# Masked products of two token tiles in one block on TensorE, with y and z a step later, and idle transposes in three waits

## The chip, the cores and the metric

The program runs on one core of a Trainium2 chip. The metric is the device time of one execution in microseconds (us), as the median of several runs. The engines are PE (TensorE; PEld is its weight load), DVE (VectorE), ACT (ScalarE), POOL (GpSimd) and SP (SyncE, which issues the DMAs).

## What is computed

Four blocks follow each other on a residual stream `x` of 1024 tokens (4 sequences of 256) by 512 columns: a retrieval attention, a layer of 8 experts, a state-space mixer, and a layer of 4 experts. The third takes most of the time. Cut to what matters:

```
proj = layernorm(x) @ in_proj_w.T                 # gate, x, B, C, dt
xBC  = silu(causal_conv4(proj's x, B, C) + conv_b)
dt   = softplus(dt + dt_bias);  x_dt = x * dt
Lmat = exp(segment_sum(A * dt))                   # per head, within a chunk of 128 tokens
M      = (C @ B.T) * Lmat
Y_diag = M @ x_dt                                 # within the chunk
Y_off  = C @ (B * decay).T @ x_dt * exp(cumsum)   # across the two chunks of a sequence
y = Y_diag + Y_off + D * x
z = y * silu(gate) * norm_w                       # and y's mean square, for the row's scale
out = (z @ out_proj_w.T) * rsqrt(mean(y^2) + eps)
```

There are 128 heads of 64 channels in 8 groups, and each group has its own B and C.

## The kernel before, in words

Every large matmul is done in three passes: each operand is split into a high and a low part of a rounded type, and high*high, high*low and low*high are added up (`three_pass`, lines 203 to 205). ACT makes a high part by a copy, POOL or DVE a low part by a subtraction.

The mixer (`ssm_block`) walks over 8 groups. A group has 16 **steps** `s`: its 16 heads are two halves of 8 (`half`), and each half passes over 8 token tiles `t` of 128 tokens. A "lead" of half a group (g = -1, steps 8 to 15) runs ahead, and the last group has no projections in its second half. Each engine has its own `step(g, s, kind)` with its instructions in a fixed order; they meet through counting semaphores. What a step holds, by engine:

- **PE**: `turn(s + 1)` transposes the next tile of x (line 1827, 4 instructions, bank 6); `diag(s)` is the masked product, 8 matmuls of 64 columns of weights, one for each head, which write to the upper and the lower half of the partitions of bank 4 in turn (line 1837; the trace has two records for each); in odd steps `across(s)` does the product over chunks for a pair of tiles (line 1854, bank 5); `project(m)` makes one of 18 projection tiles of a group, 24 matmuls of 512 columns (lines 203 to 205, banks 0 to 3 in turn); `add_up(s - 1)` multiplies z of the tile before by the output weights, 12 matmuls of 512 columns into bank 7 (lines 1865, 1866 with z's high part, line 1869 with its low part). At the end of a group `within` (line 1916) and line 1963 form C*B for the next group.
- **DVE**: adds bank 7 to the accumulator (line 1569), scales the transposed x by dt (`times_dt`, line 1580), adds three taps of the convolution where the tile has one (`taps`, line 1558), scales the product over chunks (line 1641), makes y (lines 1653, 1663), z (line 1669), and masks the decays of tile s + 2 (`mask`, line 1602).
- **ACT**: takes projection s - 1 out of its bank (line 1300 or 1308), rounds the weights of tile m + 2 (line 1288), at the second tile of a half the output weights (line 1333, which waits for the last `add_up` of the half before), makes the decays of tile s + 2 (line 1321 eight times, line 1326 once, and a table load before it), applies silu to a convolved tile (line 1312), squares y (line 1394), and makes z's high part (line 1397).
- **POOL**: the low part of the weights (line 1215) and of z (line 1236), the sums of squares (1239 to 1245), and x scaled to the end of the chunk (1225).
- **SP**: the loads. A buffer of decays is loaded again when `diag_done` says that its tile was used.

So in the kernel before the masked product, y and z of tile s stand in step s, and the product of z with the output weights in step s + 1. The tables that place the projections are these (`has_tile` leaves out what a kind of group does not have):

```python
PROJECTED = [[n] for n in range(10)] + [[10, 11], [12], [13, 14], [15], [16], [17]]
EARLY = [[-1]] + [[n] for n in range(10)] + [[11], [12], [14], [15], [16]]
LATE = [[]] * 10 + [[10], [], [13], [], [], []]
```

Before the mixer and in each expert layer a layer norm is done (`norm_tensor`, `norm_vector`, `norm_scalar`): statistics and a square root on DVE and ACT, and then for each of 8 token tiles the normalised tile is transposed on PE (line 194), and split by ACT (line 182) and DVE (line 171). Blocks are separated by a barrier of all engines.

Of the kernel before, what the change touches and what calls it, by code (L numbers as in the profile page):

```python
# [174 lines left out]
def norm_scalar(nc, act, n, xh, between=None, after=None):  # L175
# [4 lines left out]
    for t in range(NT):  # L180
# [3 lines left out]
        if after:  # L184
            after(t)

# [387 lines left out]
def experts_block(nc, sems, tag, x, xh, xl, ident, bank, w, n, *, experts, rank, top2, scaling, split_low=False,  # L574
# [5 lines left out]
    with ExitStack() as ctx:  # L580
# [30 lines left out]
        with nc.Block() as block:  # L611
# [111 lines left out]
            def _(pe):  # L723
# [22 lines left out]

                norm_tensor(nc, pe, n, after=lambda t: products(t - 1) if t >= 1 else None)
# [3 lines left out]
                base(3)  # L751
                for hf in range(2):
# [26 lines left out]
def ssm_block(nc, ctx, sems, n, x_saved, ident, bank, acc, xh, xl, xdt, w_bufs, w_in, w_dt, par, dt_bias, a_log, w_out,  # L779
              ncs_dram, ecs_dram, units_dram, ffn, out):  # L780

# [244 lines left out]

    def has_tile(kind, m):

        return kind != "last" if m >= LEAD else kind != "lead"
# [37 lines left out]
    with nc.Block() as block:  # L1067
        @block.sync
        def _(sp):
# [88 lines left out]
            def step(g, s, kind):  # L1158
# [17 lines left out]
                if s % 2 == 1 and own(kind) and ahead(kind, s + 4):  # L1176
                    sp.wait_ge(y_ready, at(g, s))
                    load_e(g, s + 4)
# [12 lines left out]
        def _(pool):  # L1191
# [36 lines left out]

            def step(g, s, kind):
                t = s % NT  # L1230
                for m in EARLY[s] + LATE[s]:
                    if has_tile(kind, m) and has_tile(kind, m + 2):
                        w_low(g, m + 2)
                if own(kind):
                    pool.wait_ge(zh_ready, at(g, s))
                    nc.gpsimd.tensor_tensor(z_l[:, s % 2, :, :], zg[:], f(z_h[:, s % 2, :, :]),  # L1236
                                            ALU.subtract).then_inc(zl_ready, 1)
                    pool.wait_ge(sq_ready, at(g, s))
                    nc.gpsimd.tensor_tensor(ysq[:, 0:2, :], ysq[:, 0:2, :], ysq[:, 2:4, :],
                                            ALU.add).then_inc(sq_pair, 1)  # L1240
                    pool.wait_ge(sq_pair, g * STEPS + (s + 1))
                    nc.gpsimd.tensor_tensor(sq_acc[:, t, :], sq_acc[:, t, :], ysq[:, 0, :],
                                            ALU.add).then_inc(sq_first, 1)
                    pool.wait_ge(sq_first, g * STEPS + (s + 1))
                    nc.gpsimd.tensor_tensor(sq_acc[:, t, :], sq_acc[:, t, :], ysq[:, 1, :],
# [560 lines left out]
        def _(pe):  # L1806
# [113 lines left out]
            def step(g, s, kind):  # L1920
                if ahead(kind, s + 1) and s != STEPS - 1:
                    turn(g, s + 1)
                if own(kind):
                    diag(g, s)
# [192 lines left out]
```

## Time and profile before

| what | us |
|---|---|
| median of 3 runs | 1738.97 (1738.46 to 1739.18) |
| the profiled execution, by its own time | 1737.69 |
| its span, first to last instruction | 1735.9 |
| PE busy in the span | 1684.0 |
| ACT, DVE, POOL busy | 1269.4, 1190.5, 732.2 |
| stretch of the 8 groups, about | 290 to 1683 |

A row of the timeline gives the start, the length, the engine, the line and the operation, what is written and read, and how many instructions were merged. A matmul's record is longer than the distance to the next, since they are pipelined: a 512-column matmul lasts some 0.39 us and the next starts 0.23 us after it. So the distances between starts are what counts on PE. PEclk is the clock granted to PE, as a share of full speed: 1.00 is 2.4 GHz and 0.50 is 1.2 GHz.

### The profile page before, as it was taken

What the parts mean: (1) busy time and instruction counts of PE and PEld (TensorE: products, weight loads), DVE (VectorE), ACT (ScalarE), POOL (GpSimd) and SP (SyncE); (2) the same over time, 40 slices, a digit from 0 to 9 for tenths busy, and PEclk for the clock granted to TensorE, in tenths of its full rate; (3) what the DMA queues carried; (4) which work ended last, traced back from release to release, by engine and by line L of the source; (5) the groups of instructions that cost most, each with busy time, mean ns of one, the idle gap of its engine ahead of it and who ended that gap; (6) DMA issues with size and microseconds to landing.
All of it is one profiled execution on the core that took longest, in us unless ns stands there. A gap on an engine that the chain in (4) does not pass through costs nothing.

```text
span 1735.9 us, 26827 instructions
## 1 busy us (share of the span) xinstructions
PE 1684.0 (97%) x9484; PEld 1378.6 (79%) x9484; DVE 1190.5 (69%) x1846; ACT 1269.4 (73%) x2171; POOL 732.2 (42%) x792
## 2 busy tenths in 40 slices
PE   6998799999999999999999999999999999999999
PEld 5876577888888888888888888888888888888877
DVE  5665676767676767667776767676767676767785
ACT  4333148987888779877987798778887889688851
POOL 3553122544344334443444444434443444344470
PEclk9998799999999999999999999999999999999999
DMA  4320225423232323332333232323232233223311
GB/s 170 109 68 1 75 65 159 122 93 105 86 112 85 117 74 111 95 109 83 113 93 107 78 110 88 116 88 109 94 110 78 86 115 104 90 79 115 105 70 49
DMA packets 98564, 166.46 MB, mean 96 GB/s; under 512 B 11616, under 2 KB 49888, under 8 KB 96768
## 3 DMA queue, kind: packets, MB, share of 16 engines
q1 hardware_dynamic: 98432, 164.75, 29.7%
q8 instruction: 76, 1.25, 0.3%
q14 instruction: 56, 0.46, 0.1%
HBM read 158.43 MB, written 6.29 MB: 95 GB/s over the span
## 4 chain that ended last, share of the span: by engine, by line
PE 81%; DVE 4%; ACT 2%; issue 1%; DVEq 0%; ACTq 0%
PE bank L203 15%; PE bank L205 15%; PE bank L204 15%; PE bank L1837 7%; PE bank L1865 7%; PE bank L1866 7%; PE bank L1869 7%; PE bank L1854 4%; PE bank L1827 3%; PE bank L1916 1%; DVE m_xc L1558 1%; DVE m_gate L1558 0%; PE bank L1845 0%; ACT m_mt L1321 0%; DVE m_xc L1492 0%
## 5 line engine op out<-in xcount | busy, mean ns | idle before, releaser
L203 PE MATMUL bank<-xh,w_h 128*128 128x512 f32 x1152 | 463.3, 402 | 3.4 <-DVE m_xc L1558 2.9
L205 PE MATMUL bank<-xh,w_l 128*128 128x512 f32 x1152 | 451.8, 392 | 0.0
L204 PE MATMUL bank<-xl,w_h 128*128 128x512 f32 x1152 | 449.4, 390 | 0.0
L1236 POOL TENSOR_TENSOR m_z_l<-m_zg,m_z_h 128x512 fp32r<-128x512 f32 x128 | 177.6, 1387 | 568.6 <-ACT m_z_h L1397 568.6
L1321 ACT ACTIVATE m_mt<-m_mt,m_unit 128x128 f32<-128x128 f32 x1024 | 312.1, 390 | 0.0
L1215 POOL TENSOR_TENSOR w_l<-w_raw,w_h 128x512 fp32r<-128x512 f32 x144 | 187.7, 1303 | 230.9 <-ACT w_h L1288 230.9
L1569 DVE TENSOR_TENSOR x<-x,bank 128x512 f32<-128x512 f32 x128 | 87.8, 686 | 264.5 <-PE bank L1869 264.5
L203 PEld LDWEIGHTS bank<-xh,w_h 128*128 128x128 f32 x1152 | 216.8, 188 | 55.7 <-issue 13.6
L205 PEld LDWEIGHTS bank<-xh,w_l 128*128 128x128 f32 x1152 | 216.5, 188 | 47.3
L1558 DVE SCALAR_TENSOR_TENSOR m_xc<-bank,m_par_conv,m_xc 128x1020 f32<-128x1020 f32 (+2 forms) x192 | 244.6, 1274 | 10.4 <-ACT m_xc L1300 5.4
L204 PEld LDWEIGHTS bank<-xl,w_h 128*128 128x128 f32 x1152 | 217.1, 188 | 41.7
L1865 PE MATMUL bank<-m_wo_h,m_z_h 128*128 128x512 f32 x512 | 203.8, 398 | 1.3 <-DVE x L1569 1.3
L1866 PE MATMUL bank<-m_wo_l,m_z_h 128*128 128x512 f32 x512 | 202.5, 396 | 0.0
L1602 DVE TENSOR_TENSOR m_mt<-m_mt,m_cb 128x1024 f32<-128x1024 f32 x128 | 156.9, 1225 | 26.1 <-ACT m_mt L1326 26.0
L1837 PE MATMUL bank<-m_mt,xdt 128*64 128x128 f32 x2048 | 140.1, 279 | 0.1
L1869 PE MATMUL bank<-m_wo_h,m_z_l 128*128 128x512 f32 x512 | 138.5, 392 | 0.0
L1326 ACT ACTIVATE m_mt<-m_mt 128x1024 f32<-128x1024 f32 x128 | 135.8, 1061 | 2.2
L1653 DVE SCALAR_TENSOR_TENSOR m_y<-m_xc,m_par_dn,bank 128x128 f32<-128x128 f32 x480 | 133.9, 342 | 1.5 <-PE bank L1837 1.5
L1837 PEld LDWEIGHTS bank<-m_mt,xdt 128*64 128x64 f32 x2048 | 109.2, 136 | 21.5 <-issue 20.5
L1580 DVE TENSOR_TENSOR xdt<-bank,m_unit 128x512 f32<-128x512 f32 x128 | 87.8, 686 | 49.5 <-issue 48.6
L1326 ACT ACT_TABLE_LOAD x93 | 119.3, 1283 | 1.6
L1865 PEld LDWEIGHTS bank<-m_wo_h,m_z_h 128*128 128x128 f32 x512 | 96.1, 188 | 24.2 <-ACT m_z_h L1397 1.3
(275 smaller groups left out, 2781.0 us busy)
## 6 DMA issues: line engine op xcount, KB each, us to landing
m_mt<-ncs_rows SPq DMA_DIRECT2D x128, 512.0 KB, 3.7
w_raw<-w_in SPq DMA_DIRECT2D x144, 256.0 KB, 3.0
m_wo_raw<-w_out_in SPq DMA_DIRECT2D x64, 256.0 KB, 5.1
m_e<-ecs_rows SPq DMA_DIRECT2D x128, 128.0 KB, 3.5
a_wo_raw<-wo_in SPq DMA_DIRECT2D x8, 1024.0 KB, 4.9
x<-x_in SPq DMA_DIRECT2D x8, 256.0 KB, 4.6
a_wq_raw<-wq_in SPq DMA_DIRECT2D x8, 256.0 KB, 4.1
x_saved<-x SPq DMA_DIRECT2D x1, 2048.0 KB, 9.1
```

The source lines that it names most:

```text
L203: nc.tensor.matmul(out, ah, bh, start=first, stop=False)
L204: nc.tensor.matmul(out, ah, bl, start=False, stop=False)
L205: return nc.tensor.matmul(out, al, bh, start=False, stop=last)
L1215: nc.gpsimd.tensor_tensor(w_l[:, m % 2, :, :], w_raw[:, m % W_BUFS, :, :], f(w_h[:, m % 2, :, :]), ALU.subtract).then_inc(w_split, 1)
L1236: nc.gpsimd.tensor_tensor(z_l[:, s % 2, :, :], zg[:], f(z_h[:, s % 2, :, :]), ALU.subtract).then_inc(zl_ready, 1)
L1321: last = nc.scalar.activation(mt[:, s % ROW_BUFS, h, :], mt[:, s % ROW_BUFS, h, :], ACT.Relu, bias=own_row)
L1326: nc.scalar.activation(slot, slot, ACT.Exp, scale=-1.0).then_inc(decay_ready, 1)
L1558: ins = nc.vector.scalar_tensor_tensor(out=dst[:, :, back:], in0=src[:, :, 0:length - back], scalar=par_conv[:, w:w + 1], in1=dst[:, :, ba ...
L1837: last = nc.tensor.matmul(bank[row:row + SP_, 4, (h // 2) * P:(h // 2 + 1) * P], xdt[:, s % 2, h * SP_:(h + 1) * SP_], mt[:, s % ROW_BUFS, ...
L1865: nc.tensor.matmul(bank[:, 7, :], z_h[:, s % 2, ct, :], wo_h[:, ct, :], start=ct == 0, stop=False)
L1866: nc.tensor.matmul(bank[:, 7, :], z_h[:, s % 2, ct, :], wo_l[:, ct, :], start=False, stop=False)
L1869: last = nc.tensor.matmul(bank[:, 7, :], z_l[:, s % 2, ct, :], wo_h[:, ct, :], start=False, stop=ct == CT - 1)
```

## The change

1. **Steps are paired** (`paired`: all but the second half of the last group). In an odd step PE does `diag(s - 1)` and `diag(s)` one after the other, the even one into bank 4 and the odd one into bank 5; in an even step it does none. `across` moves to bank 7, which it shares with `add_up`.
2. **y and z are made a step later**: DVE, ACT and POOL do tile s - 1 in step s, DVE ahead of `times_dt` and the taps, ACT after the decays but ahead of silu. `add_up(s - 1)` keeps its place in step s. In the last group's second half tile s is made in step s again; its first step makes tiles 7 and 8.
3. **The end of a group**: `within(0)`, `within(1)` and the matmuls of line 1963 stand together, between the two halves of projection 16, in step 14; step 15 does both its masked products first.
4. **POOL** makes z's low part after the first tile's weights and ahead of the second tile's, in the two steps that have two.
5. **`turn_idle`** puts transposes of the identity on PE, 30 of them ahead of the first expert layer's norm and of the mixer's norm, and 24 after `base(3)` in the first expert layer, ahead of the wait for `hw_ready`. Nothing reads them.

The diff, cut to its core:

```diff
+def turn_idle(nc, bank, ident, count, spare=7):
+    for _ in range(count):
+        nc.tensor.transpose(bank[:, spare, 0:P], ident[:], ident[:])
...
+                turn_idle(nc, bank, ident, 30)
                 norm_tensor(nc, pe, n, after=lambda t: products(t - 1) if t >= 1 else None)
                 products(NT - 1)
                 base(2)
                 base(3)
+                pe.wait_ge(a_read, NT)
+                turn_idle(nc, bank, ident, 24, spare=3)
...
+    def paired(kind, s):
+        return not (kind == "last" and s >= NT)
+
+    def masked_in(kind, s):
+        if not own(kind):
+            return []
+        if paired(kind, s):
+            return [s - 1, s] if s % 2 == 1 else []
+        return [s]
+
+    def made_in(kind, s):
+        if not own(kind):
+            return []
+        if paired(kind, s):
+            return [s - 1] if behind(kind, s - 1) else []
+        return [s - 1, s] if s == NT else [s]
...
             # SP
-                if own(kind) and ahead(kind, s + ROW_BUFS):
-                    sp.wait_ge(diag_done, at(g, s))
-                    load_rows(g, s + ROW_BUFS)
+                for done in masked_in(kind, s):
+                    if ahead(kind, done + ROW_BUFS):
+                        sp.wait_ge(diag_done, at(g, done))
+                        load_rows(g, done + ROW_BUFS)
...
             # POOL, step
-                for m in EARLY[s] + LATE[s]:
+                for m in EARLY[s]:
                     if has_tile(kind, m) and has_tile(kind, m + 2):
                         w_low(g, m + 2)
+                for made in made_in(kind, s):
+                    split_and_square(g, made)
+                for m in LATE[s]:
+                    if has_tile(kind, m) and has_tile(kind, m + 2):
+                        w_low(g, m + 2)
...
             # ACT, step: after decay(g, s + 2), ahead of silu
+                if paired(kind, s):
+                    for made in made_in(kind, s):
+                        square_and_high(g, made)
                 for m in EARLY[s]:
                     if has_tile(kind, m) and is_conv[m % TILES]:
                         silu(g, m)
...
             # DVE, step: ahead of times_dt and taps
+                if paired(kind, s):
+                    for made in made_in(kind, s):
+                        make_y(g, made)
+                        make_z(g, made)
+                    if own(kind) and s % 2 == 1:
+                        scale_across(g, s, kind)
                 if ahead(kind, s + 1) and s != STEPS - 1:
                     times_dt(g, s + 1)
...
             # PE, diag
-                pe.wait_ge(y_ready, at(g, s - 1))
+                by_tensor = g == LAST and s >= NT
+                to_bank = 4 if by_tensor else 4 + s % 2
+                pe.wait_ge(y_ready, at(g, s - 1 if by_tensor and s > NT else s - 2))
...
             # PE, step
-                if own(kind):
-                    diag(g, s)
+                for ready in masked_in(kind, s):
+                    diag(g, ready)
+                if own(kind) and s % 2 == 1:
+                    across(g, s, kind)
                 todo = [m for m in PROJECTED[s] if has_tile(kind, m)]
+                for m in todo[:1]:
+                    project(g, m, 0)
+                    if s == STEPS - 2 and kind != "last":
+                        within(0).then_inc(cb_first_done, 1)
+                        within(1).then_inc(cb_last_done, 1)
...
+                    project(g, m, 1)
```

The order on PE, in an even and the following odd step of a middle group (`m_xc` is x, `m_mt` the masked decays, `m_cb_across` and `m_xdd` the product over chunks, `m_z_l` z's low part). Before, the end of one `add_up` and the next step's first instructions, for an odd step:

```order
L1869 MATMUL bank<-m_wo_h,m_z_l 128x512 x4
L1827 MATMUL bank<-ident,m_xc 128x128 x4
L1837 MATMUL bank<-m_mt,xdt 64x128 x8
L1854 MATMUL bank<-m_cb_across,m_xdd 128x128 x4
L203 MATMUL bank<-xh,w_h 128x512
```

An even step has the same without the row of line 1854. Now, an odd step:

```order
L1953 MATMUL bank<-m_wo_h,m_z_l 128x512 x4
L1901 MATMUL bank<-ident,m_xc 128x128 x4
L1915 MATMUL bank<-m_mt,xdt 64x128 x16
L1935 MATMUL bank<-m_cb_across,m_xdd 128x128 x4
L210 MATMUL bank<-xh,w_h 128x512
```

The 8 masked matmuls of the even step have moved behind it, into one block of 16, and the even step goes from line 1901 straight to line 210.

The order on ACT, in the first group's steps 0 and 1 (`m_mt` the decays, `m_ysq` the squares, `m_z_h` z's high part, `m_wo_h` the output weights). Before, from the decays of step 0:

```order
L1321 ACTIVATE m_mt<-m_mt,m_unit 128x128 x8
L1326 ACT_TABLE_LOAD
L1326 ACTIVATE m_mt<-m_mt 128x1024
L1394 ACTIVATE m_ysq<-m_y 128x512
L1397 ACTIVATE m_z_h<-m_zg 128x512
L1308 ACT_TABLE_LOAD
L1308 ACTIVATE m_gate<-bank 128x1024
L1288 ACTIVATE w_h<-w_raw 128x512
L1333 ACTIVATE m_wo_h<-m_wo_raw,m_par_dn 128x512 x4
L1321 ACTIVATE m_mt<-m_mt,m_unit 128x128 x8
```

Now:

```order
L1365 ACTIVATE m_mt<-m_mt,m_unit 128x128 x8
L1370 ACT_TABLE_LOAD
L1370 ACTIVATE m_mt<-m_mt 128x1024
L1352 ACT_TABLE_LOAD
L1352 ACTIVATE m_gate<-bank 128x1024
L1332 ACTIVATE w_h<-w_raw 128x512
L1377 ACTIVATE m_wo_h<-m_wo_raw,m_par_dn 128x512 x4
L1365 ACTIVATE m_mt<-m_mt,m_unit 128x128 x8
L1370 ACT_TABLE_LOAD
L1370 ACTIVATE m_mt<-m_mt 128x1024
L1410 ACTIVATE m_ysq<-m_y 128x512
L1413 ACTIVATE m_z_h<-m_zg 128x512
```

z's high part of the first tile has moved behind a projection's eviction, the output weights and a whole set of decays.

## Rows read from the trace of the kernel before

**Rows 1.** Windows: engines' busy us (count), PEclk, DMA; the groups' stretch

```profile
260.00:1700.00 1440.00, 1431.77 (x8295) 1176.00 (x8296) 1010.51 (x1514) 1177.69 (x2044) 640.47 (x728) 1.00 0.31 99
```

**Rows 2.** Timeline, PE, an odd step from 902.61 and an even one from 913.42

```profile
902.61 0.60 PE L1827 MATMUL bank<-ident,m_xc 128*128 128x128 f32 x4
903.14 1.09 PE L1837 MATMUL bank<-m_mt,xdt 128*64 128x128 f32 x16
904.16 1.16 PE L1854 MATMUL bank<-m_cb_across,m_xdd 128*128 128x128 f32 x8
...
910.64 0.40 PE L1865 MATMUL bank<-m_wo_h,m_z_h 128*128 128x512 f32 x1
...
913.42 0.60 PE L1827 MATMUL bank<-ident,m_xc 128*128 128x128 f32 x4
...
915.32 0.39 PE L204 MATMUL bank<-xl,w_h 128*128 128x512 f32 x1
...
920.56 0.40 PE L1865 MATMUL bank<-m_wo_h,m_z_h 128*128 128x512 f32 x1
```

**Rows 3.** Groups by line: busy us, mean ns, idle before; the masked products

```profile
L1837 PE MATMUL bank<-m_mt,xdt 128*64 128x128 f32 x2048 | 140.1, 279 | 0.1
```

**Rows 4.** Timeline, PE: a `turn` with no masked product behind it

```profile
827.22 0.60 PE L1827 MATMUL bank<-ident,m_xc 128*128 128x128 f32 x4
...
827.89 0.39 PE L1866 MATMUL bank<-m_wo_l,m_z_h 128*128 128x512 f32 x1
```

**Rows 5.** Timeline, ACT, around the even step at 913.42

```profile
912.28 2.44 ACT L1321 ACTIVATE m_mt<-m_mt,m_unit 128x128 f32<-128x128 f32 x8
...
917.52 0.61 ACT L1397 ACTIVATE m_z_h<-m_zg 128x512 fp32r<-128x512 f32 x1
```

**Rows 6.** Timeline, PE and ACT, step 1 of a middle group

```profile
840.39 0.60 PE L1827 MATMUL bank<-ident,m_xc 128*128 128x128 f32 x4
...
840.64 2.56 ACT L1333 ACTIVATE m_wo_h<-m_wo_raw,m_par_dn 128x512 fp32r<-128x512 f32 x4 [0.66 <-issue]
...
848.35 0.62 ACT L1397 ACTIVATE m_z_h<-m_zg 128x512 fp32r<-128x512 f32 x1
```

**Rows 7.** Timeline, ACT and PE, steps 0 and 1 of the first group

```profile
301.12 1.06 ACT L1326 ACTIVATE m_mt<-m_mt 128x1024 f32<-128x1024 f32 x1
...
303.23 1.28 ACT L1308 ACT_TABLE_LOAD   x1
304.52 1.03 ACT L1308 ACTIVATE m_gate<-bank 128x1024 f32<-128x1024 f32 x1
...
309.13 0.40 PE L1865 MATMUL bank<-m_wo_h,m_z_h 128*128 128x512 f32 x1
```

**Rows 8.** Timeline, PE and ACT, step 8 of the last group

```profile
1632.20 0.60 PE L1827 MATMUL bank<-ident,m_xc 128*128 128x128 f32 x4
...
1634.66 0.48 PE L1865 MATMUL bank<-m_wo_h,m_z_h 128*128 128x512 f32 x1
...
1634.28 1.06 ACT L1326 ACTIVATE m_mt<-m_mt 128x1024 f32<-128x1024 f32 x1
```

**Rows 9.** Windows, as rows 1: the three stretches at half clock ahead of the groups

```profile
143.70:153.80 10.10, 6.64 (x25) 5.85 (x26) 4.71 (x17) 2.21 (x4) 0.27 (x8) 0.50 0.01 3
...
181.20:187.90 6.70, 6.33 (x18) 4.45 (x17) 4.42 (x8) 1.20 (x2) 0.00 (x0) 0.50 0.00 0
...
205.10:218.70 13.60, 8.14 (x29) 6.28 (x30) 11.16 (x29) 6.64 (x11) 4.76 (x8) 0.50 0.73 269
```

**Rows 10.** Windows of line 1988 alone (transposes): PE busy, PEld busy, PEclk, DMA, GB/s

```profile
1686.50:1689.80 3.30, 2.77 (x13) 2.78 (x14) 0.50 0.00 0
1689.90:1693.30 3.40, 0.46 (x4) 0.22 (x2) 1.00 0.00 0
```

**Rows 11.** Timeline, DVE and PE: behind the barrier ahead of the first expert layer

```profile
143.26 0.64 DVE L150 BATCH_NORM_AGGREGATE e0n_mv<-e0n_stats 128x2 f32<-128x6 f32 x8 [0.30 <-PEq L268]
...
146.60 0.69 PE L194 MATMUL bank<-ident,e0n_xn 128*128 128x128 f32 x2 [6.32 <-DVE e0n_xn L161]
```

More of the change, by code:

```diff
@@ L1175, in step @@
                         load_tile(g, m + 5)
-                if s % 2 == 1 and own(kind) and ahead(kind, s + 4):
-                    sp.wait_ge(y_ready, at(g, s))
-                    load_e(g, s + 4)
+                for made in made_in(kind, s):
+                    if made % 2 == 1 and ahead(kind, made + 4):
+                        sp.wait_ge(y_ready, at(g, made))
+                        load_e(g, made + 4)
                 if own(kind) and t == 3 and (half == 0 or kind != "last"):
@@ L1671, in step @@
+                    dve.wait_ge(cb_last_done, g + 2)
+                    cb_evict(1)
+                if not paired(kind, s):
+                    for made in made_in(kind, s):
+                        if made % 2 == 1 and made == s:
+                            scale_across(g, made, kind)
+                        make_y(g, made)
+                        make_z(g, made)
                 if kind == "lead" and s == STEPS - 1:
@@ L1858, in add_up @@
             def add_up(g, s):
+                g, s = g + s // STEPS, s % STEPS
+                half, t = divmod(s, NT)
                 pe.wait_ge(zh_ready, at(g, s))
                 pe.wait_ge(acc_added, at(g, s - 1))
-                half, t = divmod(s, NT)
+                if s % 2 == 0 and not (g == LAST and s >= NT):
+                    pe.wait_ge(off_ready, pair(g, s + 1))
                 for ct in range(CT):
@@ L1915, in within @@
                     cols = slice((part * CT + i) * P, (part * CT + i + 1) * P)
[L1916 removed]
+                    last = nc.tensor.matmul(bank[:, 5 - part, i * P:(i + 1) * P], b_cm[:, cols], c_cm[:, cols],
                                             start=True, stop=True)
@@ L1922, in step @@
                     turn(g, s + 1)
-                if own(kind):
-                    diag(g, s)
-                if s == STEPS - 2 and kind != "last":
-                    pe.wait_ge(silu_done, conv_at(g, C_TILE))
-                    pe.wait_ge(off_ready, pair(g, s - 1))
-                    within(0).then_inc(cb_first_done, 1)
-                if own(kind) and s % 2 == 1 and s != STEPS - 1:
-                    across(g, s)
-                todo = [m for m in PROJECTED[s] if has_tile(kind, m)]
@@ L1949, in step @@
+                if s == STEPS - 1 and kind != "last":
+                    pe.wait_ge(cb_across_ready, g + 2)
+                    turn(g, s + 1)
                 if behind(kind, s - 1):
@@ L1956, in step @@
                         project(g, m, 1)
-                if s == STEPS - 2 and kind != "last":
-                    pe.wait_ge(cb_ready, g * 2 + 3)
-                    within(1).then_inc(cb_last_done, 1)
-                    pe.wait_ge(xdt_ready, at(g, s + 1))
-                    for b in range(SEQS):
-                        first = b * CHUNKS * P
-                        last = nc.tensor.matmul(bank[:, 6, b * P:(b + 1) * P], b_cm[:, first:first + P],
-                                                c_cm[:, first + P:first + 2 * P], start=True, stop=True)
-                    last.then_inc(cb_across_done, 1)
             def sums(hf):
```

187 lines of the change are left out of this document (99 added, 88 removed).

## The prediction

> **What bounds the kernel now.** I first read the windows of the long stretch of the 8 groups: PE is busy for 1431.8 of 1440 us, at the full clock (PEclk 1.00), with ACT at 1177.7 and DVE at 1010.5 [rows 1]. So in that stretch the program is as long as PE's own stream, and a wait of another engine matters only where it stops PE. Then the timeline of PE, where the distances between starts are to be read. A masked product starts 0.53 us after the start of the 4 transposes ahead of it, and what follows it starts 1.02 us after it [rows 2]. The groups by line say that one block is busy for 140.1 / 128 = 1.09 us from its first start to its last end; one record lasts 0.28 us, so the last one starts 0.82 us after the first [rows 3]. The other 0.20 us of the 1.02 are a pause behind the block, and the transposes, whose own spacing is (0.60 - 0.27) / 3 = 0.11 us, take 0.53 us to the block where 0.44 would do: a pause of 0.1 ahead of it. These pauses look like busy time on the page. They are paid twice in each pair of steps, and the change pays them once. Ahead of the groups the clock is the thing to see: three stretches, of 10.1, 6.7 and 13.6 us, ran at 0.50, each behind or in a wait of PE [rows 9].
>
> **The change part by part.**
>
> *The pairing, in the groups.* An even step had from the start of its transposes to its second full matmul 915.32 - 913.42 = 1.90 us, with the masked product between [rows 2]; without one the same two are 827.89 - 827.22 = 0.67 us apart [rows 4]. So the product costs 1.23 us in a step of its own. Behind another one it costs its 8 heads. By rows 3 a head takes 0.82 / 7.5 = 0.109 us, so 0.87 us; at worst it pays a full pause again, 1.02 us [rows 2], at best only 0.82. That saves 0.36 us a pair, with ends of 0.21 and 0.41. I take 0.35, nearest to the row of 128 blocks, which is what a longer block repeats. There are 60 pairs (8 in each of 7 groups, 4 in the last). The first lies ahead of a wait that is priced below, so 59 x 0.35 = **-20.6 us** (-12.4 to -24.2). The C*B products in one place and `across` in bank 7 change no instruction's size; their waits (for y of tile 13, and for the accumulator of tile s - 2) are done by DVE in the first 3 us of a step, and PE asks later. I cost them at nothing; the half projection of 2.8 us ahead of `within` is their cover.
>
> *y and z a step later.* This is the wait that the change adds. `add_up(s - 1)` now uses z of the same step. What is queued behind it on PE is everything. In an odd step it starts 910.64 - 902.61 = 8.03 us after the transposes, and 8.9 with the second product; in an even step 920.56 - 913.42 = 7.14, and 5.9 without the product [rows 2]. ACT has z's high part when the decays are done: its decays start 1.14 us before an even step, and z is finished 918.13 - 913.42 = 4.7 us into it [rows 2, 5]. The margin is 1.2 us in a plain even step and 4 in an odd one. Two places are tighter. In steps 1 and 9 ACT first makes the output weights, which wait for PE's last `add_up`: z ends 848.97 - 840.39 = 8.6 us into the step, against 8.9 [rows 6]. And behind an odd step with a convolved tile silu, which now comes last, holds up the next eviction; I estimate z at 5.5 against 5.9. I cost these at nothing with margins of 0.3 and 0.4; if the cover is gone, each tenth beyond it at some 30 such steps is 3 us.
>
> *First group.* Here ACT lags from the lead, and the margin is not there. Its decays of step 0 end at 302.18 [rows 7]. Then come, now, a table load 1.28, an eviction 1.03, a weight copy 0.61 (as the copy in rows 5), the output weights 2.56 [rows 6], decays 2.44 [rows 5], 1.28 and 1.06 [rows 7], a square and z at 0.61 each: 11.5 us, less some 0.5 by which neighbours overlap, so 313.2. PE began this `add_up` at 309.13 before [rows 7]: **+4.1 us** (3.5 to 4.6), whatever the lead gains on PE ahead of it (about a us, by the C*B products in one place).
>
> *Last group, step 8.* Its `add_up(7)` began 2.46 us into the step; there is no projection ahead of it, and z of tile 7 was there. Now it is made in this step, behind decays that end at 1635.34, so at the earliest at 1636.5 against 1634.66 [rows 8]: 1.9 us. y and z on DVE make it about 2.2, and the output weights, which wait for this `add_up`, start later by as much: **+2.5 us** (1.9 to 4).
>
> *Idle turns.* At full clock 30 take 3.3 us, at half clock, by rows 10 at 2.77 / 13 = 0.213 each, 6.4. In the first place PE sat idle for 6.3 us to 146.60, but can begin only behind the barrier, at 143.3, so the turns just fit at full clock and overrun by up to 3 at half [rows 11]. What can come back: with 6.64 us of PE busy at half clock at most 3.3, in the second place (6.33 busy) at most 3.2, in the third (8.14 busy, but DVE busy for 11.16 of 13.6, so PE is not what ends it) at most 2 [rows 9]. Below nothing: an overrun, 1 us each. I take 2.0 + 2.5 + 0.5 = **-5.0 us**. The middle one is the surest: its wait is cut to about a us. In the first the clock may have dropped before the barrier lets the turns begin, and then they run at half clock until it is back. In the third the norm that follows leaves PE mostly waiting, so the clock can fall again.
>
> That transposes bring the clock back at all the trace shows: from 1686.5 to 1689.8 PE did nothing but 13 of them, at 0.50, and the next window is at 1.00 [rows 10]. The Trainium skill, "TensorE: Matmul & The Clock Gate", Part 4 on the transpose, says the opposite (in my words): the full clock does not engage for transposes, which do not count as a busy PE. By that rule the turns would give nothing, and the sum would be 5 us higher. The measured row decides, for this kind of transpose.
>
> **The sum.** -20.6 + 4.1 + 2.5 - 5.0 = -19.0 on the profiled execution's 1737.69: 1718.7. The median stands 1.3 higher at 1738.97, so I predict **1720.0 us**. A difference of 0.2% (3.5 us) is about what a measurement of this kernel can tell from none.
>
> **The rivals.**
>
> *The turns give nothing* (the clock falls in the waits in spite of them, or transposes don't hold it). For it: in the third stretch PE worked off 29 instructions, most of them transposes of the norm, with pauses between, and stayed at 0.50 all the while [rows 9]. Against: rows 10. The time is 1720 + 5 = 1725. Chance 0.13. The Trainium skill's sentence on the transpose, told above, would make this rival the forecast.
>
> *The margins of 0.3 and 0.4 us don't hold.* z comes 0.3 late at some 30 steps: 9 us, so 1729. For it: ACT, DVE and POOL share more of the step than before. Against: the margins are worked out from undisturbed rows, and plain steps have over a us. Chance 0.12.
>
> *All goes better*: the block saves 0.41, the turns give 7, the first wait is shorter. 1720 - 3.5 - 2 - 1 = 1713.5. Chance 0.10.
>
> *ScalarE becomes the bound (slower).* Every z now hangs, within its own step, on eviction, decays, square and copy on ACT, at a margin of 1.2 us in even steps. Should ACT fall behind by more, each even step waits for ACT, whose eviction then waits for PE: a ring that never catches up. The gain of 19 us is gone at 0.3 us of waiting in each of 60 even steps, that is z 1.5 us later than I work out; at 2 us later, 60 x 0.8 = 48, so 1749. Against: ACT still has 260 us free in 1440 [rows 1]. Chance 0.03.
>
> *Pauses come back*: the 16 products wait between the two tiles for a semaphore and pay 1.02 [rows 2], so 59 x 0.21 = 12.4, and with the rest 1728. Chance 0.08. That it does nothing at all (within 0.2%): 0.02.
>
> **How the numbers follow.** The forecast has 0.52. The better case ends at about 1713 and the two near 1729 bound the other side; 1712 to 1730 leaves the ring, no change, and tails: under 0.2. Faster by over 0.2%: 0.95; within: 0.02; slower: 0.03.
>
> **What would show it.** In the profile after: blocks of 32 records of the masked product with one start-to-start distance of about 1.9 us to `across`; 0.67 from transposes to the second full matmul in even steps; a wait of PE of some 5 us, for z's high part, at the first `add_up` of the first group, one of 2 in step 8 of the last, and none above 0.5 elsewhere; PEclk 1.00 where 181.2 to 187.9 had 0.50. A long list of PE waits for z's high part in all groups would show the forecast wrong, and a 0.50 behind the turns would show that part wrong.

## The result and the profile after

| | before | after |
|---|---|---|
| median of 6 runs each, us | 1739.03 (1738.3 to 1742.21) | 1733.35 (1730.79 to 1734.61) |
| profiled execution, own time / span | 1737.69 / 1735.9 | 1734.61 / 1732.9 |
| ratio of the two, 95% interval | | 0.9965 (0.9955 to 0.9976) |

It is faster by 5.7 us, where 19 had been forecast, and 1733.35 lies outside the range of 1712 to 1730.

The pairing itself is there. Timeline of PE after (start, length, line, what is written and read, count): an odd step and the even step behind it.

```profile
900.92 1.97 PE L1915 MATMUL bank<-m_mt,xdt 128*64 128x128 f32 x32
902.82 1.16 PE L1935 MATMUL bank<-m_cb_across,m_xdd 128*128 128x128 f32 x8
903.73 0.47 PE L210 MATMUL bank<-xh,w_h 128*128 128x512 f32 x1
...
912.08 0.60 PE L1901 MATMUL bank<-ident,m_xc 128*128 128x128 f32 x4
912.43 0.48 PE L210 MATMUL bank<-xh,w_h 128*128 128x512 f32 x1
912.75 0.39 PE L211 MATMUL bank<-xl,w_h 128*128 128x512 f32 x1
```

The two products are one block of 32 records: 1.90 us from its start to `across`, against 1.02 for one before [rows 2], so the second costs 0.88. In the even step 0.67 us lie between the transposes and the second full matmul, as in a turn alone [rows 4]. And the group of the masked products, from the page after, answers to [rows 3], with 126.8 us for 140.1:

```profile
L1915 PE MATMUL bank<-m_mt,xdt 128*64 128x128 f32 x2048 | 126.8, 276 | 0.0
```

Then the waits of PE after, from the lead to the tail (what waited, for what: us in total, times, longest). Before, such a list had no wait of `add_up` for z's high part.

```profile
PE bank L1949 <- ACT m_z_h L1413: 6.7, 2, 4.8
...
PE bank L1999 <- DVE m_y L1688: 1.1, 7, 0.2
```

Two waits for z in all, where two had been foretold, and 7 small ones, one in each group, ahead of C*B. The first of the large ones, in the first group, on PE's timeline (in brackets the idle time and what ended it):

```profile
313.18 0.68 PE L1949 MATMUL bank<-m_wo_h,m_z_h 128*128 128x512 f32 x1 [4.76 <-ACT m_z_h L1413]
313.65 0.63 PE L1950 MATMUL bank<-m_wo_l,m_z_h 128*128 128x512 f32 x1
314.08 0.63 PE L1949 MATMUL bank<-m_wo_h,m_z_h 128*128 128x512 f32 x1
...
317.62 0.60 PE L1901 MATMUL bank<-ident,m_xc 128*128 128x128 f32 x4
```

It ends at 313.18, where 313.2 had been worked out. That the clock times agree so well is in part luck: attention ended 2.7 us later in this execution and the idle transposes gave back 2.9, so ACT stood where it had stood before. What holds is the length of ACT's chain, from the end of the decays (302.08) to this matmul 11.1 us, with 11.0 worked out. Behind it the matmuls start 0.43 us apart instead of 0.23: the clock has fallen. The windows of after say so (engines' busy us, count; then PEclk, DMA share, GB/s), here and at two other places, and they show the first idle transposes and the stretch that was the middle one [rows 9]:

```profile
146.00:149.50 3.50, 3.50 (x17) 3.50 (x18) 2.61 (x17) 1.42 (x2) 0.33 (x8) 0.51 0.04 9
149.50:152.00 2.50, 2.47 (x23) 2.23 (x21) 0.64 (x2) 0.43 (x1) 0.00 (x0) 1.00 0.00 0
152.00:204.00 52.00, 46.95 (x272) 39.88 (x272) 28.24 (x62) 8.59 (x20) 9.04 (x1) 1.00 0.00 1
204.00:211.00 7.00, 5.92 (x28) 5.95 (x29) 4.37 (x19) 1.49 (x2) 1.56 (x5) 0.51 0.50 142
...
313.20:316.80 3.60, 3.60 (x9) 2.83 (x10) 0.14 (x1) 3.60 (x10) 3.44 (x5) 0.53 0.00 0
1627.30:1630.90 3.60, 3.58 (x9) 2.85 (x10) 2.32 (x3) 0.00 (x0) 3.40 (x4) 0.53 0.62 127
1705.90:1709.40 3.50, 3.50 (x16) 2.96 (x15) 1.12 (x2) 0.60 (x1) 0.00 (x0) 0.51 0.18 69
```

The drop at 181 is gone; the other two are shorter. The wait ahead of 1627.3 is the foretold one in step 8 of the last group; in step 9, behind it, the matmuls of `add_up` come in pairs with gaps, each pair waiting for a part of the output weights:

```profile
1624.19 1.16 PE L1922 MATMUL bank<-m_xc,w_raw 128*128 128x128 f32 x8
1627.32 0.69 PE L1949 MATMUL bank<-m_wo_h,m_z_h 128*128 128x512 f32 x1 [1.97 <-ACT m_z_h L1413]
...
1635.12 0.48 PE L1949 MATMUL bank<-m_wo_h,m_z_h 128*128 128x512 f32 x1
1635.44 0.40 PE L1950 MATMUL bank<-m_wo_l,m_z_h 128*128 128x512 f32 x1
1635.91 0.51 PE L1949 MATMUL bank<-m_wo_h,m_z_h 128*128 128x512 f32 x1
```

Now the program can be cut at marks that every trace has on PE: the last product of attention (A), the transposes in step 2 of the first group (B), those in step 8 of the last (C), those in step 10 (D), and the end. All lengths in us, from the starts on the timelines of the profiled executions:

| stretch | before | after | difference | forecast |
|---|---|---|---|---|
| start to A, no change in the code | 139.89 | 142.60 | +2.7 | 0 |
| A to B: turns, lead, first wait | 172.03 | 175.02 | +3.0 | -0.9 |
| B to C: 59 pairs | 1320.28 | 1305.01 | -15.3 | -20.6 |
| C to D: steps 8 and 9 of the last group | 11.61 | 16.50 | +4.9 | +2.5 |
| D to the end | 92.08 | 93.76 | +1.7 | 0 |
| sum | 1735.89 | 1732.89 | -3.0 | -19.0 |

The first row is chance: the same attention ended between 139.59 and 143.99 us in the 12 executions profiled in this study. I take the last row for chance too. The change leaves these steps as they were; after has a stretch at half clock there (1705.9 us, in the windows above) where before has the full clock; the kernel before with idle transposes alone had 93.53; and before's 92.08 is the shortest of the 12, with 92.48 and 92.57 for two kernels below whose tail is that of the changed one. The three stretches that the change touches differ by -7.4 us, against the -19.0 forecast. The medians differ by -5.7, and the 95% interval of their ratio is -7.8 to -4.2 us. Before's profiled execution lay 1.3 us below its median and after's 1.3 above, which accounts for 2.6 of the 4.4 us in the two chance rows; the other 1.8 are not accounted for.

The 5.3 us missing in the groups are found by laying the distances between the transposes of successive tiles beside each other, for the six groups between (each distance was the same in all six within 0.04 us):

| distances | before | after | difference |
|---|---|---|---|
| a plain pair of steps | 20.74 | 20.41 | -0.33 |
| the pair with tile 8's transposes | 20.74 | 20.68 | -0.06 |
| the pair around C*B, end of the group | 23.44 | 23.54 | +0.10 |

So two of the eight pairs of a group gain nothing. At the first, the transposes wait. At the second, C*B waits for y. Timelines of PE and ACT at one of the first, and of POOL, DVE and PE at one of the second:

```profile
543.91 1.09 PE L1953 MATMUL bank<-m_wo_h,m_z_l 128*128 128x512 f32 x4
545.04 0.66 PE L1901 MATMUL bank<-ident,m_xc 128*128 128x128 f32 x4
545.62 1.97 PE L1915 MATMUL bank<-m_mt,xdt 128*64 128x128 f32 x32
...
543.92 1.06 ACT L1356 ACTIVATE m_xc<-m_xc 128x1024 f32<-128x1024 f32 x1 [1.02 <-DVE m_xc L1609]
...
630.55 1.30 POOL L1255 TENSOR_TENSOR w_l<-w_raw,w_h 128x512 fp32r<-128x512 f32 x1
...
630.98 1.42 DVE L1688 TENSOR_TENSOR m_y<-m_y,m_e 128x512 f32<-128x512 f32 x1
...
632.00 0.39 PE L212 MATMUL bank<-xh,w_l 128*128 128x512 f32 x1
632.55 2.02 PE L1999 MATMUL bank<-m_gate 128*128 128x128 f32 x16 [0.15 <-DVE m_y L1688]
```

Tile 8 is the first of the second half, and its x must be through silu. ACT's silu ends at 543.92 + 1.06 = 544.98, and the transposes start 0.06 later; in a plain step they would have started 0.2 earlier. Silu waits for DVE's taps, which the change put behind y and z. The page books no idle time there, since the matmuls ahead are still running in its model. At C*B it books 0.15, but the start of C*B is 0.55 us after the last full matmul, where a full matmul starts 0.23 after another. Both waits cost more than they show.

Why y of tile 13 is late can be read from the rows too, though no run tested it. DVE's last addition for it (line 1688) takes 0.69 us where POOL does not make the low part of a weight (line 1255) at the same time; it takes 0.78 to 0.90 where the two overlap by 0.23 to 0.35 us, 1.00 to 1.02 where they overlap by 0.45 to 0.48, and 1.42 to 1.44 at each of the 7 places ahead of C*B, where they overlap by 0.88 or 0.89.

### The profile page after: what moved, and what is told of

It reads as the page before. It is cut to its first block, busy times and chain, and to the rows that moved or that the text cites. A ratio compares the mean times of both kernels' runs of the same rounds, so it can differ in the third digit from the quotient of the medians.

```text
span 1732.9 us, 27059 instructions
## 1 busy us (share of the span) xinstructions
PE 1679.2 (97%) x9568; PEld 1388.4 (80%) x9568; DVE 1204.7 (70%) x1846; ACT 1265.2 (73%) x2171; POOL 754.7 (44%) x792
## 4 chain that ended last, share of the span: by engine, by line
PE 80%; DVE 5%; ACT 2%; issue 1%; DVEq 0%; ACTq 0%
PE bank L210 14%; PE bank L212 14%; PE bank L211 14%; PE bank L1949 7%; PE bank L1950 7%; PE bank L1915 7%; PE bank L1953 7%; PE bank L1935 4%; PE bank L1901 3%; PE bank L1999 1%; DVE m_xc L1609 1%; DVE m_y L1688 1%; ACT m_mt L1365 1%; DVE m_y L1678 1%; DVE m_gate L1609 0%
## 5 line engine op out<-in xcount | busy, mean ns | idle before, releaser
L1609 DVE SCALAR_TENSOR_TENSOR m_xc<-bank,m_par_conv,m_xc 128x1020 f32<-128x1020 f32 (+2 forms) x192 | 244.4, 1273 | 14.8 <-ACT m_xc L1344 10.2
L1653 DVE TENSOR_TENSOR m_mt<-m_mt,m_cb 128x1024 f32<-128x1024 f32 x128 | 161.5, 1262 | 34.6 <-ACT m_mt L1370 28.1
L1356 ACT ACTIVATE m_xc<-m_xc 128x1024 f32<-128x1024 f32 x64 | 68.0, 1062 | 115.6 <-DVE m_xc L1609 115.4
L1915 PE MATMUL bank<-m_mt,xdt 128*64 128x128 f32 x2048 | 126.8, 276 | 0.0
```

The costliest lines, as they stand in the source:

```text
L1609: ins = nc.vector.scalar_tensor_tensor(out=dst[:, :, back:], in0=src[:, :, 0:length - back], scalar=par_conv[:, w:w + 1], in1=dst[:, :, ba ...
L1915: last = nc.tensor.matmul(bank[row:row + SP_, to_bank, (h // 2) * P:(h // 2 + 1) * P], xdt[:, s % 2, h * SP_:(h + 1) * SP_], mt[:, s % ROW ...
```

## The experiments

Times are medians; the ratio is to the runs of the kernel before on the same chip, whose median was 1738.65 to 1739.69 us. The changed kernel itself was not run again beside them, so "below the change" sets medians of different chips side by side. The theory to test: the sum was right in the plain steps, and what is missing lies at five places. The rivals: the pairing is worth less than worked out; the clock takes it back; the later y and z cost in all steps.

**Idle turns, taken away and alone.** The changed kernel without its three runs of transposes:

```diff
-                turn_idle(nc, bank, ident, 30)
...
-                turn_idle(nc, bank, ident, 24, spare=3)
...
-            turn_idle(nc, bank, ident, 30)
```

> The changed kernel without its three runs of idle transposes. My theory from the two traces: at the dt projection (about 248 us) both kernels stand at the same time although attention ended 2.7 us later in the changed one, so the turns gave 2.8 us, not the 5.0 I had forecast: expected 1733.35 + 2.8 = 1736.2 us, with the 0.50 stretches back at about 144 to 154, 181 to 188 and 205 to 219, and at 248 us some 2.8 later than with turns when counted from the end of attention. Rival A, they gave the 5.0 of the forecast: 1738.4. Rival B, they gave nothing (the turns at half clock overran what they brought): 1733.4.

The kernel before with them alone:

> The kernel before with the three runs of idle transposes and nothing else. By my theory (2.8 us, all of it ahead of the groups): 1739.03 - 2.8 = 1736.2 us. Rival A (5.0): 1734.0. Rival B (nothing): 1739.0. If this one and the run without turns do not agree in size, the turns and the rest of the change are not independent.

Measured: 1736.97 us without (10 runs, ratio 0.9989, 0.9980 to 0.9999), 3.6 above the change; 1737.07 alone, ratio 0.9990 (0.9981 to 0.9999), 1.7 below before. On the traces A to B is 177.80 against 175.02 with them (2.8), and 168.91 against 172.03 (3.1). So they give some 3 us, between no gain and the forecast's 5. By stretches, the middle one gave 2.0 us, the first 0.7, the third nothing within 0.5.

**Pairing undone**, but for the last pair of a group:

```diff
+            if s < STEPS - 2:
+                return [s]
             return [s - 1, s] if s % 2 == 1 else []
```

> The changed kernel with each masked product in its own step again (the last pair of a group stays, since C*B needs both its banks): 52 pairs behind the first wait are undone. y and z stay a step later, C*B stays in one place. Theory: 52 x 0.348 = 18.1 us back, less the 0.27 us that each of 7 groups now loses ahead of the first transposes of the second half (PE arrives earlier there because step 6 got shorter), so +16.2: 1749.5 us, and that late silu no longer stops PE. Rival A: a product behind another saves nothing and the gain came from C*B or from the turns: about 1733 to 1736. Rival B: y and z a step later make waits of their own in unpaired steps too, over 0.2 us in most steps: above 1755.

Measured: 1760.87, ratio 1.0128 (1.0109 to 1.0148): 27.5 us slower than the change, and 22 slower than the kernel before. My figure missed by 11, and rival B is right in its sign, though not "in most steps". Plain pairs are back at 20.74, as before. But in each group four steps are longer than before: steps 1 and 9 by 0.70 us each, step 13 by 0.39 and step 14, with C*B, by 0.18. PE's waits in the groups of this kernel, and one of them with ACT's work ahead of it:

```profile
PE bank L1951 <- ACT m_z_h L1415: 6.2, 14, 0.4
PE bank L2001 <- DVE m_y L1690: 1.9, 7, 0.3
```

```profile
496.69 0.39 PE L212 MATMUL bank<-xh,w_l 128*128 128x512 f32 x1
497.52 0.50 PE L1951 MATMUL bank<-m_wo_h,m_z_h 128*128 128x512 f32 x1 [0.44 <-ACT m_z_h L1415]
```

```profile
489.15 2.56 ACT L1379 ACTIVATE m_wo_h<-m_wo_raw,m_par_dn 128x512 fp32r<-128x512 f32 x4 [1.29 <-issue]
...
496.86 0.61 ACT L1415 ACTIVATE m_z_h<-m_zg 128x512 fp32r<-128x512 f32 x1
```

The 14 waits are in steps 1 and 9, where ACT makes the output weights first: the places whose margin the prediction gave as 0.3 us (in the changed kernel it is 0.33). It holds only because the second product in an odd step puts `add_up` 0.9 us later. With one product it is gone, and a wait booked at 0.44 lengthens the step by 0.70 (11.51 for 10.81). The length of a group is 181.69 us here, 179.69 before and 177.64 after. So the rest of the change, y and z a step later above all, costs 2.0 us a group without these seven pairs, and pairing them gives 4.05 back, where 7 x 0.35 would be 2.45: part of its gain is the cover that it makes for its own delay.

**The clock held in the two waits:**

```diff
+                if kind == "first" and s == 1:
+                    pe.wait_ge(off_ready, pair(g, s))
+                    turn_idle(nc, bank, ident, 40)
+                if kind == "last" and s == NT:
+                    pe.wait_ge(off_ready, pair(g, s - 1))
+                    pe.wait_ge(acc_added, at(g, s - 2))
+                    turn_idle(nc, bank, ident, 18)
```

> The changed kernel with idle transposes also in the two waits it made: 40 ahead of the first group's first product with the output weights (wait 4.76 us), 18 ahead of the last group's in step 8 (wait 2.25). They change no wait. Theory: what these waits cost beyond their own length is the clock that fell to 0.50 behind each (313.3 to 316.7 and 1627.5 to 1630.9), 1.65 and 1.55 us; held up, both go: 1733.35 - 3.2 = 1730.1 us and no 0.50 at those two places. Rival A: the clock falls in spite of the transposes: no change, or up to 1 us more by overrun: 1733.4 to 1734.4. Rival B: the fall is a matter of chance and not of the wait: some executions show it elsewhere, difference under 1 us.

Measured: 1731.55, ratio 0.9958 (0.9943 to 0.9972), 1.8 below the change. A to B fell by 1.5 (173.53): the clock behind the first wait is worth that. PE's timeline there:

```profile
305.43 4.53 PE L192 MATMUL bank<-ident 128*128 128x128 f32 x40
310.35 0.50 PE L1949 MATMUL bank<-m_wo_h,m_z_h 128*128 128x512 f32 x1 [0.40 <-ACT m_z_h L1413]
310.69 0.39 PE L1950 MATMUL bank<-m_wo_l,m_z_h 128*128 128x512 f32 x1
```

In the last group the half clock went as well, step 8 fell from 9.13 to 7.58 us, and step 9 grew from 7.36 to 8.95: nothing was gained. The end of the two steps is not set by PE there, so its clock was no cost. In the changed kernel, something else is late in step 9, and ACT's timeline shows what:

```profile
1631.66 0.63 ACT L1410 ACTIVATE m_ysq<-m_y 128x512 f32<-128x512 f32 x1 [4.40 <-POOL m_sq_acc L1280]
...
1632.72 2.54 ACT L1377 ACTIVATE m_wo_h<-m_wo_raw,m_par_dn 128x512 fp32r<-128x512 f32 x4
```

ACT's square of tile 8 waits 4.40 us for POOL's sums of tile 7, and the output weights that `add_up` needs in step 9 come only behind it.

**The tiles at both ends in their own steps** (tiles 0 and 1 of the first group, tile 7 of the last):

```diff
-        if paired(kind, s):
+        if paired(kind, s) and not (kind == "first" and s < 2):
             return [s - 1, s] if s % 2 == 1 else []
...
+    def early_made(kind, s):
+        if not own(kind) or not paired(kind, s) or (kind == "first" and s <= 2):
+            return []
+        return [s - 1] if behind(kind, s - 1) else []
+
+    def late_made(kind, s):
+        if kind == "first" and s < 2:
+            return [s]
+        if kind == "last" and s == NT - 1:
+            return [s]
+        return [] if paired(kind, s) else [s]
```

> The changed kernel, except that tiles 0 and 1 of the first group and tile 7 of the last are masked, and made into y and z, in their own steps as before (pairing given up for one pair). Theory: the two waits go with all that hangs on them. First group: 4.05 us of wait and 1.65 of half clock behind it, less 0.35 for the pair, 5.3. Last group: 3.8 in step 8 (wait 2.25, half clock 1.55) and 1.1 in step 9, where the output weights came late because ACT's square of tile 8 waited for POOL's sums of tile 7; 4.9. Together 10.2: 1723.1 us, with step 9 of the last group back at 6.3 us (it was 7.4, and 8.95 when the wait was filled with idle transposes). Rival A: ACT's lag of the first group is only passed on to the next step: 2 us less gained, 1725. Rival B: the late z was not the cause, PE waits there for something else: no gain, 1733.

Measured: 1726.97, ratio 0.9930 (0.9914 to 0.9945), 6.4 below the change where 10.2 had been expected. The first group gave what it should: A to B 168.78, 6.2 less, of which B to C takes 0.9 back. The last did not. Step 8 is at 5.33, as before, but step 9 at 10.13 instead of 6.3. Timeline of PE in step 9, then ACT in step 7:

```profile
1621.66 0.60 PE L1908 MATMUL bank<-ident,m_xc 128*128 128x128 f32 x4
...
1628.00 0.48 PE L1956 MATMUL bank<-m_wo_h,m_z_h 128*128 128x512 f32 x1 [2.74 <-DVE m_wo_l L1646]
```

```profile
1610.56 0.61 ACT L1423 ACTIVATE m_z_h<-m_zg 128x512 fp32r<-128x512 f32 x1
1616.05 0.63 ACT L1420 ACTIVATE m_ysq<-m_y 128x512 f32<-128x512 f32 x1 [4.88 <-POOL m_sq_acc L1290]
```

Two tiles are made in one step here, and the square of the second may not overwrite the first before POOL has summed it. ACT stood 4.88 us in that wait with the eviction and the decays queued behind it, and so the output weights of the second half came late. That is the same chain as in the changed kernel, one step earlier.

**Two orders on TensorE** (the transposes of tile 8 behind the products; the half of C*B whose bank is free first):

```diff
-                if ahead(kind, s + 1) and s != STEPS - 1:
+                if ahead(kind, s + 1) and s != STEPS - 1 and s != NT - 1:
                     turn(g, s + 1)
                 for ready in masked_in(kind, s):
                     diag(g, ready)
+                if ahead(kind, s + 1) and s == NT - 1:
+                    turn(g, s + 1)
...
-                            pe.wait_ge(y_ready, at(g, s - 1))
+                            pe.wait_ge(y_ready, at(g, s - 2))
...
-                        within(0).then_inc(cb_first_done, 1)
                         within(1).then_inc(cb_last_done, 1)
+                        if own(kind):
+                            pe.wait_ge(y_ready, at(g, s - 1))
+                        within(0).then_inc(cb_first_done, 1)
```

> The changed kernel with two orders on TensorE changed: in step 7 of a group the transposes of tile 8 come behind the two masked products (they waited for the silu of a convolved tile), and of the two halves of C*B the one whose bank is free earlier comes first (the other waits for y of tile 13). Theory: these two waits are where the groups lost 0.27 + 0.3 us of the pair's gain, in 7 groups each: 4.0 us, 1729.4. Rival A: the transposes behind the products bring a pause of their own and only the C*B part counts: 1731.2. Rival B: what a pair lost there is not a wait but the price of the block in that place: 1733.4.

Measured: 1726.18, ratio 0.9925 (0.9907 to 0.9942). B to C is 1299.86, 5.15 less than after: the pair with tile 8 is at 20.39 and the pair around C*B at 23.13, 0.3 and 0.4 less in each group. Window of this kernel over the groups: PE has no idle time left.

```profile
330.00:1600.00 1270.00, 1270.00 (x7396) 1055.22 (x7395) 912.13 (x1336) 1058.91 (x1832) 587.45 (x647) 1.00 0.32 99
```

The median fell by 7.2, where 4.0 had been expected; the trace shows 5.2 in the groups, and the rest is within what the runs of one kernel differ. B to C is now 20.4 less than before, against the forecast's 20.6.

This trace also says something of the clock. In step 8 of its last group PE waits the same 1.97 us for z's high part, and here the clock stays up behind it:

```profile
1620.70:1623.60 2.90, 2.89 (x13) 2.31 (x13) 1.60 (x3) 0.00 (x0) 2.78 (x3) 1.00 0.52 82
```

Step 8 is then 7.57 us instead of 9.13, and it falls to 0.50 at 1630.4 instead, in step 9, which takes 10.18.

**Idle transposes ahead of the barriers too:**

```diff
+                turn_idle(nc, bank, ident, 24, spare=0)
...
+                turn_idle(nc, bank, ident, 24, spare=2)
```

> The changed kernel with 24 more idle transposes on TensorE at the end of attention and at the end of the first experts, ahead of the barrier that PE waits at for 3 us each time. Theory: the clock fell at the end of these waits, so the 30 turns behind them ran at 0.50 and ended 1.7 and 2.5 us after the norm's first tile was ready; with the clock held they end in time: 1733.35 - 3.5 = 1729.9 us, PEclk 1.00 from 130 to 220 us. Rival A: the clock falls at another place of the norms instead, where PE waits in between: under 1 us gained. Rival B: DVE and ACT, not the turns, end the wait of the norm: 1733.4.

Measured: 1732.07, 1.3 below the change, with an interval of its ratio (0.9944 to 0.9972) that holds both. The windows answer the question of the clock:

```profile
140.50:147.00 6.50, 6.14 (x56) 5.80 (x53) 5.31 (x22) 1.49 (x2) 0.41 (x9) 1.00 0.02 5
...
199.00:206.00 7.00, 6.48 (x56) 5.94 (x54) 6.11 (x21) 1.49 (x2) 1.57 (x5) 1.00 0.15 38
```

Nothing but transposes ran on PE in these two stretches, and the clock stayed. But it fell to 0.50 at 181 and near 212, in the work behind, so rival A holds in part: 1.2 us were gained from A to behind the third norm, and 0.6 of them are left at B.

**All three together.**

> All three together. If the places are independent: 1733.35 - 10.2 - 4.0 - 3.5 = 1715.6 us, which is also about what the forecast of 1720 would have been had its cover held everywhere. Rival: they are not independent (ACT's lag in the first group takes what PE gains ahead of it, 3 us): 1719.

Measured: 1720.41, ratio 0.9892 (0.9876 to 0.9908). The rival's 1719 is nearer than 1715.6, but not for its reason: from A to B this kernel takes 167.42 us, 1.4 less than with the tiles in their own steps alone, so ACT's lag took nothing there. What is missing is in the last group, where step 9 took 11.74 us, since PE came to it earlier and the weights did not.

**ACT's order in the last group.** All three together, and in the last group ACT does its part for tile 7 behind the eviction of step 8 and no longer in step 7. `z_high` and `square` are the two halves of that part:

```diff
-                for made in late_made(kind, s) if own(kind) else []:
+                for made in late_made(kind, s) if own(kind) and not (kind == "last" and s == NT - 1) else []:
                     square_and_high(g, made)
...
+                if kind == "last" and s == NT:
+                    z_high(g, s - 1)
+                    square(g, s - 1)
```

> All three changes together (1720.4), and in the last group ACT makes z's high part of tile 7 and squares its y only behind the eviction of step 8. Theory: in step 7 ACT stood idle for 4.9 us for POOL's sums of tile 6 and so came late with the output weights of the second half (step 9 of the last group took 10.1 to 11.7 us instead of 6.3). With the eviction and its table load in that idle time ACT is 3 us earlier: step 9 some 8, 1717.5. Rival A: ACT is late by its own load (decays of tile 10, two tiles to square), not by the idle time: under 1 us, 1720. Rival B: add_up of tile 7 now waits for z: 2 us and the clock with it, 1723.

Measured: 1718.71, ratio 0.9878 (0.9858 to 0.9897). Step 9 is at 7.62, 4.1 less than with all three. The median is only 1.7 below, and the intervals of the two ratios overlap, so it is the trace that shows this gain. The wait for the weights on PE's timeline:

```profile
1614.39 0.47 PE L1967 MATMUL bank<-m_wo_h,m_z_h 128*128 128x512 f32 x1 [0.23 <-DVE m_wo_l L1657]
```

**Idle transposes in the tail**, 18 ahead of the last norm, added to the kernel just measured:

```diff
             sums(1)
+            turn_idle(nc, bank, ident, 18, spare=0)
```

> The kernel just named with 18 idle transposes ahead of the last norm's first transposes, where PE waits for 2.3 us and the clock fell to 0.50 in every execution profiled so far. 18 take 2.0 us at full clock. Theory: 3.3 us of PE's work at half clock come back as 1.6: 1.6 below the kernel without them. Rival: in this norm ACT and DVE set the pace and not PE (16 transposes, each tile waited for): 0 to 0.5.

Measured: 1715.02, ratio 0.9865 (0.9848 to 0.9882), 3.7 below the one without, with intervals that overlap. The traces do not carry that: D to the end is 93.47 against 93.92, 0.45 less. PE's timeline shows why the rival is right on the norm:

```profile
1660.30 2.16 PE L192 MATMUL bank<-ident 128*128 128x128 f32 x18
1662.73 2.02 PE L2083 MATMUL bank<-ident,m_wo_raw 128*128 128x128 f32 x16 [0.27 <-DVE m_wo_raw L1815]
1665.30 0.39 PE L210 MATMUL bank<-xh,m_xeh 128*128 128x256 f32 x1 [0.54 <-DVE m_xel L1820]
```

The 16 transposes take 2.0 us, 3.1 in the version before, and then PE waits for DVE's low parts. With four runs each, and those of one kernel over 5 us apart, how the other 3 us came about stays open. This last version is 23.6 us faster than the kernel before and 18.3 faster than the change.

## Why the prediction was wrong

The direction was right, the size not. By its own steps:

- **The saving of a pair, -0.35 us: right.** Plain pairs gave 0.33, and the second product cost 0.88 for 0.87. With the two small waits gone the 59 pairs gave 20.4 for 20.6.
- **"I cost them at nothing" (C*B and `across`), "the half projection of 2.8 us ahead of `within` is their cover": this failed.** PE asks 3.2 us into the step, and y of tile 13 is there 3.4 us into it, since DVE's last addition took 1.42 us, beside POOL's work, and not 0.69 (the row at 630.98). I had put it within 3 us. That costs 0.45 us in each of 7 groups. Together with the late silu, which the prediction saw as a delay of ACT's next eviction and not as one of the transposes of tile 8 (0.29 us in each group), that is 5.2 us. In both I looked for a wait of PE of over half a microsecond, and none is that long.
- **First group, +4.1: ACT's chain right to 0.1 us, the price of the wait not.** It costs 1.65 more, since the clock falls behind it. The prediction counted half clock in waits that were there, and never asked it of the two waits that the change makes.
- **Last group, step 8, +2.5: mis-sized, it is 4.9.** The wait for z was right, `add_up` starts 2.2 us later in the step. The forecast's step itself had the chain in it ("the output weights [...] start later by as much") and did not follow it. In step 9 the weights wait for ACT, ACT for POOL's sums of the tile made a step late. That the clock fell there too costs nothing, as holding it showed.
- **Idle turns, -5.0: it is -2.9.** The middle one gave 2.0 for 2.5. The first gave 0.7 for 2.0: its transposes ran 17 of 30 at half clock and ended 1.6 us too late. The third gave nothing for 0.5.
- **The margins of 0.3 and 0.4 us held** (0.33 in steps 1 and 9, 0.36 and 0.44 in steps 4 and 6 of a middle group), and the rival that they would not is refuted for the changed kernel; unpaired, they fail at once. ScalarE as a ring did not come. Its price was also added up wrongly: 1720 and 48 make 1768 and not 1749, which takes the gain of 19 off twice. It bounds nothing in the range.

From the traces, against the forecast: 5.3 in the groups, 1.7 behind the first wait, 2.4 in the last group, 2.1 in the turns: 11.5 of the 13.3 us by which the medians missed it. The other 1.8 are inside the interval of the measurement and have no place in the traces. Each place was then changed and moved in the traces as this says, with two exceptions: in the last group the first remedy only moved the chain, and the transposes that held the clock ahead of the turns gave 0.6 at B, since it fell elsewhere.

## What to carry to other kernels

Where one engine is busy for 99% of a stretch, a wait that lengthens one step of sixteen by 0.3 us takes away all that one pair of steps saves, and the page hardly books it: lay the distances between the same mark in successive steps of both traces beside each other. When a result is made a step later, write down for the first, the last and the heaviest step who makes it, and what that engine does ahead of it; the plain step says nothing of them. And where a change makes a new wait, add what may stand behind it: the clock, but only if that engine sets the end. Last, a row's length is that of its own place: an instruction moved beside another engine's work can take twice as long, as the addition ahead of C*B did.

## What was not expected of the hardware

- The granted clock fell behind a wait of PE of 2 us, as in the window from 1627.3 us, and not only behind the long ones [rows 9]. But not always: behind the same wait it stayed at 1.00 with pairing undone and with the two orders (the window from 1620.7 us), and also behind the 2.74 us in step 9 with the tiles in their own steps. Behind the wait of 3.7 to 4.8 us in the first group it fell in all five kernels that have it unfilled.
- A wait that a profile books at 0.44 us lengthened its step by 0.70, and one of 0.15 by some 0.3. In the first case the matmul behind the wait starts 0.83 us after the last one ahead of it (496.69 to 497.52) instead of 0.23, and the next one 0.34 behind it.
- Transposes alone keep the clock at 1.00 (windows 140.5 and 199.0 us above) and bring it back (the window from 149.5 us after). The Trainium skill, "TensorE: Matmul & The Clock Gate", Part 4, has it that the full clock does not engage for a transpose. These rows disagree, for transposes of 4-byte data by a matmul with the identity.
- The time of the same attention, at the start of the program, differs by up to 4.4 us between executions. Of the 2.7 us between before and after, 2.3 are there at the same matmul near 20 us (18.37 and 20.67). Before it, the full matmuls of after start 0.43 us apart, until 19.7 us, where those of before start 0.23 apart from 15.6 us on: the clock rose later. The Trainium skill's same page, Part 1, says that the moment at which the clock rises varies from run to run. What makes it rise late in one execution and not in another, no run here shows.
